# Feed-forward stages of a four-layer metaformer: residual additions moved to GpSimd, the result's rounding to VectorE, a second bank for the centred product in the last stage, zero products on TensorE at the start

## The chip, the cores and the metric

The kernel runs on one core of a Trainium2 chip. The metric is the device time of one execution in microseconds (us), lower is better. Engines are named as in the profile: PE is TensorE (PEld its weight loads), DVE VectorE, ACT ScalarE, POOL GpSimd, SP the engine that issues most DMAs here.

## The reference, cut to what matters

The input is 16 images of 24 channels on 56 x 56 pixels, float32. Four layers follow one another. Each has a mixer (attention in windows, a state-space block, a scan in four directions, a row LSTM) and a feed-forward block:

```python
x = x + mixer(_ln_c(x))                 # normalised over the channels of a pixel, eps 1e-6
t = _to_tokens(x)
h = relu(_qlinear(_ln_t(t), W1, b1))    # 24 -> 96; _ln_t: over the channels too, eps 1e-5
t = t + _qlinear(h, W2, b2)             # 96 -> 24
# _qlinear: operands rounded to 8-bit floats (5 exponent bits, 2 of mantissa), product and sum to float16
```

## The kernel before

All four layers are one program. `x` (tile `all_x`) stays in SBUF for the whole run: four groups of 24 channels lie on partitions 0, 32, 64 and 96, and four images follow one another along each, 12,544 columns in all. `feed_forward_phase` runs once for each layer, after its mixer, which has left its result in device memory (`mixed`, or `by_image` in layer 2). Each feed-forward stage walks over the 12,544 columns in 32 chunks of N = 392. The first three stages (layers 1 to 3) end with the channel norm for the next mixer, which goes to `normed` in device memory; the fourth stage (`last`) stores `x` itself as the output.

The engines each run an order written out by hand, in slots: slot s works on the first step of chunk s, the hidden layer of chunk s-1, the second product of chunk s-2 and the closing norm of chunk s-3. Slots 0 to 2 and the last four are written out, the ones between are a hardware loop over four slots. Semaphores count chunks: a wait for `added` c+1 waits for the addition of chunk c. The steps by their lines:

- SP stores what is finished (`store`, four DMAs, lines 231 and 237) and then loads the mixer's result for the chunk that is six further on (`load`, line 220, four DMAs of 36.8 KB, `AHEAD` = 6, in four buffers).
- DVE adds the mixer's result to `x` (`add_mixed`, L308). PE subtracts the mean (`subtract_mean`, L418, into PSUM tile `xc_ff`, or `xc_ln` for the closing norm). ACT squares (L362), PE averages (`variance`, L425, into `var_ff`, or `ps_y` for the closing norm), ACT takes a logarithm (L368) and an exponential (L372). DVE multiplies and rounds to 8 bits (`quantize`, L285).
- PE makes the hidden layer in two halves (L436), ACT rounds each to float16 (`round_hidden`, L379), DVE adds the bias and rectifies (`rectify`, L292) and rounds to 8 bits (`quantize_hidden`, L303).
- PE makes the second product (L449, into `ps_y`), ACT rounds it to float16 (`round_result`, L386), DVE adds the bias (`add_bias`, L321) and adds the result to `x` (`update`, L314).
- In stages 1 to 3, PE, ACT, PE, ACT, ACT and DVE (`norm`, L330, tile `staged`) make the closing norm of chunk s-3.

GpSimd does nothing in these stages. PE waits for the weights and for all preparations before its first product.

Of the kernel before, what the change touches and what calls it, by code (L numbers as in the profile page):

```python
# [125 lines left out]
AHEAD = 6  # L126


def feed_forward_phase(nc, x, mixed_dram, normed_dram, out_dram, w, st, layer, by_image=False):
# [6 lines left out]
    with ExitStack() as ctx:  # L136
# [37 lines left out]
        ff, ln = st.ff, st.ln  # L174

        all_loads = (layer + 1) * 6 * 16
        preps = 12
# [24 lines left out]
        with nc.Block() as block:  # L202
            @block.sync
            def _(sp):

                sp.dma_start(centre[:], w["centre"]).then_inc(st.weights_in, 16)
                sp.dma_start(average[:], w["average"]).then_inc(st.weights_in, 16)
                sp.dma_start(w1f[:], w["ff_w1"][layer]).then_inc(st.weights_in, 16)
                sp.dma_start(w2f[:], w["ff_w2"][layer]).then_inc(st.weights_in, 16)
                sp.dma_start(b1f[:], w["ff_b1"][layer]).then_inc(st.weights_in, 16)  # L210
                sp.dma_start(b2f[:], w["ff_b2"][layer]).then_inc(st.weights_in, 16)

                def load(j, k, b):
# [3 lines left out]
                    for g in range(G):  # L217
                        rows = (mixed_dram[j + g * J, :, k * N:(k + 1) * N] if by_image
                                else mixed_dram[c + g * CHUNKS])
                        sp.dma_start(group_rows(mixed[b], g), rows  # L220
                                     ).then_inc(st.mixed_in[b], 16)

# [18 lines left out]
                sp.wait_ge(st.prepared, prep0 + 1)  # L241
                for k in range(AHEAD):
                    load(0, k, k % UNROLL)
# [13 lines left out]
            def _(dve):  # L257

                for b in range(UNROLL):

                    cleared = dve.memset(mixed[b][:], 0.0)
# [12 lines left out]
                dve.wait_ge(st.prepared, prep0 + 11)  # L274
# [4 lines left out]
                def quantize(c):  # L279
# [5 lines left out]
                    dve.tensor_tensor(xq[:], xc["ff"][:, 0:N], rstd["ff"][:], ALU.mult,  # L285
# [19 lines left out]
                def add_mixed(c, turn, u):  # L305

                    dve.wait_ge(st.mixed_in[u], (turn + (layer * (CHUNKS // UNROLL) + 1)) * G * 16)
                    dve.tensor_tensor(x[:, bass.ds(c * N, N)], x[:, bass.ds(c * N, N)],  # L308
                                      mixed[u][:], ALU.add).then_inc(ff["added"], 1)

                def update(c):

                    dve.wait_ge(ff["biased"], c + 1 + fb)
                    dve.tensor_tensor(x[:, bass.ds(c * N, N)], x[:, bass.ds(c * N, N)],  # L314
                                       yb[:], ALU.add).then_inc(ff["updated"], 1)
# [20 lines left out]
                def slot(s, turn, u, on):  # L336
                    if on[0]:
                        quantize(s)
# [17 lines left out]
            def _(act):  # L356
# [31 lines left out]
                def slot(s, turn, u, on):  # L388
# [4 lines left out]
                    if on[2]:  # L393
                        round_result(s - 2)
# [1966 lines left out]
```

## Time and profile before

| | us |
|---|---|
| median of 3 runs | 3848.09 (3843.79 to 3852.31) |
| the profiled execution's own time | 3854.38 |
| its span in the profile | 3852.5 |
| first feed-forward stage, first to last quantize (start to start) | 835.0 to 999.9 |
| second | 2413.7 to 2577.3 |
| third, within 0.1 us as long as the second | 3157.6 to 3321.1 |
| fourth | 3675.5 to 3839.1 |

The profile is one execution of the whole program, and its span leaves out 1.9 us that the execution's own time has. The share of busy time of an engine over the span says little here, since the four stages that the change touches take about a fifth of it; what matters is how far apart the slots of a stage are, and which chain of waits sets that distance.

### The profile page before, as it was taken

How to read it: one execution, taken by the hardware profiler on the slowest of the kernel's cores; microseconds unless marked ns; L12 is line 12 of the kernel's file. 1: busy time of each engine (PE TensorE's matmuls, PEld its weight loads, DVE VectorE, ACT ScalarE, POOL GpSimd, SP SyncE). 2: the span in 40 equal slices, each digit the busy share in tenths (PEclk: the TensorE clock that was granted, in tenths of full speed). 3: DMA queues.
4: the chain of work that ended last, by engine and by line, in shares of the span. 5: the costliest groups of instructions: out<-in, count | busy, mean ns of one | idle time of the engine just before them, and what ended most of it. 6: DMA issues, size and time to landing. Idle time of an engine off the chain costs nothing. (4 is left out here: it accounts for less than half of the span.)

```text
span 3852.5 us, 71476 instructions
## 1 busy us (share of the span) xinstructions
PE 3198.3 (83%) x20904; PEld 1809.4 (47%) x20904; DVE 2774.0 (72%) x4460; ACT 2555.0 (66%) x4684; POOL 1635.8 (42%) x1502
## 2 busy tenths in 40 slices
PE   5799999978677898989999765877888858688865
PEld 2688888854233343434444321333433324377722
DVE  2566666657408999989999994666999967544456
ACT  4455555559698988989898642785665629644456
POOL 0233333310047888989898863003766730000000
PEclk9899999989898999999999997998999979899979
DMA  4100000012256657574766522220000002410022
GB/s 96 28 14 14 14 14 14 14 27 59 75 140 186 160 165 197 145 200 134 208 160 188 149 64 73 49 51 22 22 21 20 18 22 58 94 39 17 17 54 53
DMA packets 210810, 298.02 MB, mean 77 GB/s; under 512 B 75034, under 2 KB 195150, under 8 KB 210258
## 3 DMA queue, kind: packets, MB, share of 16 engines
q1 hardware_dynamic: 201066, 286.08, 28.7%
q10 hardware_dynamic: 9576, 10.08, 1.1%
q8 instruction: 59, 0.97, 0.1%
q14 instruction: 109, 0.89, 0.1%
HBM read 193.93 MB, written 102.03 MB: 77 GB/s over the span
## 5 line engine op out<-in xcount | busy, mean ns | idle before, releaser
L1586 POOL TENSOR_TENSOR mam_hc<-mam_h,mam_cs 128x896 f32<-128x896 f32 x336 | 703.1, 2093 | 188.0 <-DVE mam_h L1551 87.0
L1551 DVE TENSOR_TENSOR_SCAN mam_h<-mam_a,mam_kept,mam_dbx 128x448 f32<-128x448 f32 x672 | 738.4, 1129 | 24.4 <-ACT mam_a L1437 23.3
L1318 PE MATMUL mam_ps_y<-mam_hc,mam_ident 128*128 128x448 f32 x1344 | 570.3, 558 | 133.1 <-POOL mam_hc L1586 132.9
L1987 POOL TENSOR_TENSOR scan_ch<-scan_h,scan_cs 128x392 f32<-128x392 f32 x256 | 339.8, 1346 | 399.6 <-DVE scan_h L1931 320.6
L1437 ACT ACTIVATE mam_a<-mam_ft,mam_a_neg 128x448 f32<-128x448 f32 x672 | 410.6, 660 | 81.0 <-DVE mam_h L1551 80.3
L1318 PEld LDWEIGHTS mam_ps_y<-mam_hc,mam_ident 128*128 128x128 f32 x1344 | 249.0, 193 | 433.4 <-POOL mam_hc L1586 224.0
L1538 DVE TENSOR_TENSOR mam_dbx<-mam_ps_u,mam_bs 128x448 f32<-128x448 f32 x672 | 381.7, 613 | 35.6 <-DMA mam_bs<-dram_bc 35.6
L766 POOL TENSOR_TENSOR att_prob<-att_prob,att_share 128x588 f32<-128x588 f32 x128 | 151.7, 1185 | 452.0 <-DVE att_share L951 452.0
L418 PE MATMUL f_xc_ff<-all_x,f_centre 128*128 (+1 forms) x256 | 125.9, 575 | 133.1 <-DVE all_x L308 133.1
L886 ACT ACTIVATE att_pt<-att_ps_t 128x512 f32<-128x512 f32 x128 | 76.5, 598 | 209.9 <-PE att_ps_t L827 209.9
L379 ACT ACTIVATE f_h<-f_hid 96x784 f16<-96x784 f32 x256 | 207.1, 811 | 0.0
L1819 PE MATMUL scan_ps_merged<-scan_ch,scan_w_merge 64*128 64x392 f32 x1024 | 203.7, 532 | 4.0 <-POOL scan_ch L1987 3.8
L867 ACT ACTIVATE att_keys<-att_ps_keys 24x392 f32<-24x392 f32 x384 | 186.9, 487 | 22.5 <-PE att_ps_keys L795 19.5
L1807 PE MATMUL scan_ps_in<-scan_xin,scan_w_in 128*128 128x392 f32 x512 | 189.7, 514 | 6.5 <-ACT scan_rest L1880 4.6
L837 PE MATMUL att_ps_out<-att_pt,att_vals 128*24 128x49 f32 x2048 | 189.5, 208 | 2.1 <-ACT att_pt L886 2.1
L839 PE MATMUL att_ps_out<-att_pt,att_vals 128*24 128x49 f32 x2048 | 187.3, 207 | 0.0
L2121 PE MATMUL lstm_ps<-lstm_hs,lstm_w_h 64*128 64x224 f32 x1344 | 143.1, 358 | 50.8 <-DVE lstm_hs L2202 50.8
L803 PEld LDWEIGHTS att_ps_vals<-att_nvals,att_xw 128*64 128x64 f32 x4096 | 130.5, 138 | 75.5 <-issue 75.5
L957 DVE TENSOR_SCALAR att_result<-att_ps_out,att_b_out 24x392 f32<-24x392 f32 x128 | 78.3, 612 | 116.5 <-PE att_ps_out L839 116.5
L814 PE MATMUL att_ps_scores<-att_keys,att_xw 128*64 128x147 f32 x2048 | 157.2, 295 | 2.0 <-ACT att_keys L867 2.0
L1931 DVE TENSOR_TENSOR_SCAN scan_h<-scan_decay_by_column,scan_h,scan_drive_by_column 128x392 f32<-128x392 f32 x112 | 156.6, 1398 | 0.2
L2121 PEld LDWEIGHTS lstm_ps<-lstm_hs,lstm_w_h 64*128 64x128 f32 x1344 | 123.5, 185 | 70.6 <-DVE lstm_hs L2202 70.2
(216 smaller groups left out, 7361.8 us busy)
## 6 DMA issues: line engine op xcount, KB each, us to landing
mam_taps<-normed SPq DMA_DIRECT2D x1008, 43.5 KB
mam_bs<-dram_bc SPq DMA_DIRECT2D x28, 896.0 KB, 14.7
mam_cs<-dram_bc SPq DMA_DIRECT2D x28, 896.0 KB, 16.6
mam_ft<-dram_steps SPq DMA_DIRECT2D x42, 448.0 KB, 4.8
normed<-f_staged SPq DMA_DIRECT2D x384, 38.1 KB
f_mixed<-mixed SPq DMA_DIRECT2D x384, 36.8 KB
dram_gs<-mam_gs SPq DMA_DIRECT2D x56, 224.0 KB, 2.1
mam_gt<-dram_gs SPq DMA_DIRECT2D x56, 224.0 KB, 2.7
```

The lines of the kernel that those rows point to most:

```text
L379: act.activation(h16[:, 2 * a:2 * a + 2, :], hid[a][0:HID, :, 0:N], ACT.Copy).then_inc(ff["hidden16"], 1)
L837: pe.matmul(ps_out[0:C, cols], vals[p][:, win, 0:C], pt[p][:, q, 64 * half:64 * half + T], start=True, stop=False)
L839: mm = pe.matmul(ps_out[0:C, cols], vals[p][:, win, C:2 * C], pt2[p][:, q, 64 * half:64 * half + T], start=False, stop=True)
L1318: mm = pe.matmul(ps_y[p % 2][:, 0:MT], ident[:], hc[t % 2][:, i, :], start=False, stop=(t % 8 == 7 and i == 1))
L1437: act.activation(a[t % 3][:, i, :], ft[p % 2][:, 0, :], ACT.Exp, scale=a_neg[:, at:at + 1]).then_inc(decays, 1)
L1538: dve.tensor_tensor(dbx[:, i, 0:MT], ps_u[:, 0:MT], bs[:, 2 * pair + i, :], ALU.mult).then_inc(driven, 1)
L1551: dve.tensor_tensor_scan(h[:, n % 8, :], a[t % 3][:, i, :], dbx[:, i, 0:MT], kept[:, at:at + 1], ALU.mult, ALU.add).then_inc(scanned, 1)
L1586: pool.tensor_tensor(hc[t % 2][:], h[:, row:row + 2, :], cs[:, 2 * pair:2 * pair + 2, :], ALU.mult).then_inc(weighed, 1)
L1807: pe.matmul(ps_in[i][:, 0:N], w_in[:, i, :], xin[p][:, :, 1:SIDE + 1], start=True, stop=True).then_inc(projected, 1)
L1819: mm = pe.matmul(ps[:, 0:N], w_merge[rows, n, :], ch[rows, n, :], start=(n == 0), stop=(n == DIRS - 1))
L1987: pool.tensor_tensor(out, hd, in_order(cs, 1 - half, d, k), ALU.mult).then_inc(weighed, 1)
L2121: mm = pe.matmul(ps[p][:, pair, half, 0:W], w_h[lanes, tap, pair, :], hs[lanes, :, y, tap:tap + SIDE], start=False, stop=(tap == 2))
```

## The change

Four edits, all in `feed_forward_phase`:

- The two additions to `x` move from DVE to GpSimd: `add_mixed` for chunks 0 to 3, then for each chunk c `update(c)` followed by `add_mixed(c + 4)`.
- `round_result` moves from ACT to DVE, just ahead of `add_bias`.
- In the last stage, where `xc_ln` has no other use, the centred product of even chunks goes to `xc_ff` and of odd chunks to `xc_ln`, and it waits for the quantize of the chunk before the last one (`held` = 1) in place of the last one.
- PE multiplies a tile of zeros (`squares_ln`, cleared by GpSimd, 128 x 128 by 128 x 392, float32) into `ps_y`: five times at its start, twice after the first variance, and twice at the end of slots 0 and 1. It then waits for the two constant matrices alone ahead of the first centred product, and SP issues these and chunk 0's load ahead of the weights.

```diff
+AHEAD_ADDED = 4
+WARM_UP = 5
+        fronts = (xc["ff"], xc["ln"]) if last else (xc["ff"], xc["ff"])
...
+                sp.dma_start(centre[:], w["centre"]).then_inc(basis_in, 16)
+                sp.dma_start(average[:], w["average"]).then_inc(basis_in, 16)
+                sp.wait_ge(st.prepared, prep0 + 1)
+                load(0, 0, 0)
+                sp.dma_start(w1f[:], w["ff_w1"][layer]).then_inc(st.weights_in, 16)
...
-                def add_mixed(c, turn, u):
-
-                    dve.wait_ge(st.mixed_in[u], (turn + (layer * (CHUNKS // UNROLL) + 1)) * G * 16)
-                    dve.tensor_tensor(x[:, bass.ds(c * N, N)], x[:, bass.ds(c * N, N)],
-                                      mixed[u][:], ALU.add).then_inc(ff["added"], 1)
...
+                def round_result(c):
+
+                    dve.wait_ge(ff["summed"], c + 1 + fb)
+                    dve.tensor_copy(y16[:], ps_y[:, 0:N]).then_inc(ff["summed16"], 1)
...
+            @block.gpsimd
+            def _(pool):
+                pool.memset(squares["ln"][:], 0.0).then_inc(warm, 1)
+
+                def add_mixed(c):
+
+                    pool.wait_ge(st.mixed_in[c % UNROLL],
+                                 (c // UNROLL + (layer * (CHUNKS // UNROLL) + 1)) * G * 16)
+                    pool.tensor_tensor(x[:, c * N:(c + 1) * N], x[:, c * N:(c + 1) * N],
+                                       mixed[c % UNROLL][:], ALU.add).then_inc(ff["added"], 1)
+
+                def update(c):
+
+                    pool.wait_ge(ff["biased"], c + 1 + fb)
+                    pool.tensor_tensor(x[:, c * N:(c + 1) * N], x[:, c * N:(c + 1) * N],
+                                       yb[:], ALU.add).then_inc(ff["updated"], 1)
+
+                for c in range(AHEAD_ADDED):
+                    add_mixed(c)
+                for c in range(CHUNKS):
+                    update(c)
+                    if c + AHEAD_ADDED < CHUNKS:
+                        add_mixed(c + AHEAD_ADDED)
...
-                def round_result(c):
-
-                    act.wait_ge(ff["summed"], c + 1 + fb)
-                    reached(act, ff["biased"], c + fb)
-                    act.activation(y16[:], ps_y[:, 0:N], ACT.Copy).then_inc(ff["summed16"], 1)
...
+                def multiply_zeros(times):
+                    for _ in range(times):
+                        pe.matmul(ps_y[:, 0:N], squares["ln"][:, 0:P], squares["ln"][:],
+                                  start=True, stop=True)
...
-                    reached(pe, s[reader], c + base)
-                    pe.matmul(xc[name][:, 0:N], centre[:], x[:, bass.ds(c * N, N)],
+                    held = int(last)
+                    if base > 0 or not isinstance(c, int) or c > held:
+                        pe.wait_ge(s[reader], c + base - held)
+                    to = fronts[u % 2] if name == "ff" else xc[name]
+                    pe.matmul(to[:, 0:N], centre[:], x[:, bass.ds(c * N, N)],
                               start=True, stop=True).then_inc(s["centred"], 1)
```

On VectorE, one slot of the hardware loop in stages 1 to 3 stands before as follows (L308 and L314 are the two additions; ISA and REGISTER_ALU rows are address arithmetic).

```order
L285 TENSOR_TENSOR f_xq<-f_xc_ff,f_rstd_ff 128x392
L308 ISA
L308 TENSOR_TENSOR all_x<-all_x,f_mixed 128x392
L290 REGISTER_ALU
L292 TENSOR_SCALAR f_hr<-f_h,f_b 96x784
L321 TENSOR_SCALAR f_yb<-f_y,f_b 128x392
L314 ISA
L314 TENSOR_TENSOR all_x<-all_x,f_yb 128x392
L290 REGISTER_ALU
L292 TENSOR_SCALAR f_hr<-f_h,f_b 96x784
L302 MEMSET f_gate 128x1
L303 CAST f_h<-f_hr 96x1568
```

The same slot on VectorE after the change.

```order
L292 TENSOR_TENSOR f_xq<-f_xc_ff,f_rstd_ff 128x392
L297 ISA
L299 TENSOR_SCALAR f_hr<-f_h,f_b 96x784
L315 CAST f_y<-f_ps_y 128x392
L39 REGISTER_ALU
L321 TENSOR_SCALAR f_yb<-f_y,f_b 128x392
L297 REGISTER_ALU
L299 TENSOR_SCALAR f_hr<-f_h,f_b 96x784
L309 MEMSET f_gate 128x1
L310 CAST f_h<-f_hr 96x1568
```

Both additions are gone, and one rounding from PSUM (`f_y<-f_ps_y`) has come in between the first rectify and the bias. GpSimd, which had no instruction here, begins a stage after the change like this (its own row order).

```order
L354 MEMSET f_squares_ln 128x392
L360 TENSOR_TENSOR all_x<-all_x,f_mixed 128x392 x4
L366 TENSOR_TENSOR all_x<-all_x,f_yb 128x392
L360 TENSOR_TENSOR all_x<-all_x,f_mixed 128x392
L366 TENSOR_TENSOR all_x<-all_x,f_yb 128x392
L360 TENSOR_TENSOR all_x<-all_x,f_mixed 128x392
```

The addition of chunk c+4 stands right behind the update of chunk c, so each of the two is queued behind what the other waits for. On PE the start of a stage after the change is this (L426 are the zero products, one row for each run of them).

```order
L426 MATMUL f_ps_y<-f_squares_ln 128x392 x5
L441 MATMUL f_xc_ff<-all_x,f_centre 128x392
L448 MATMUL f_var_ff<-f_squares_ff,f_average 128x392
L426 MATMUL f_ps_y<-f_squares_ln 128x392 x2
L441 MATMUL f_xc_ff<-all_x,f_centre 128x392
L448 MATMUL f_var_ff<-f_squares_ff,f_average 128x392
L426 MATMUL f_ps_y<-f_squares_ln 128x392 x2
L456 MATMUL f_hid<-f_gate_bf 128x2
```

Before, the centred product was PE's first instruction of a stage; now five products of zeros stand ahead of it, and two more stand between a chunk's variance and the hidden layer of the chunk before it, in slots 0 and 1.

## Rows read from the trace of the kernel before

**Rows 1.** Timeline, stage 1, one slot: start, length, engine, line [idle before it]
```profile
901.44 0.57 DVE L285 TENSOR_TENSOR f_xq<-f_xc_ff,f_rstd_ff 128x392 fp8e5<-128x392 f32 x1
...
901.92 0.56 DVE L308 TENSOR_TENSOR all_x<-all_x,f_mixed 128x392 f32 x1
...
902.62 0.92 PE L418 MATMUL f_xc_ff<-all_x,f_centre 128*128 x2 [0.50 <-DVE all_x L308]
...
904.22 0.90 PE L425 MATMUL f_var_ff<-f_squares_ff,f_average 128*128 128x392 f32 x2
...
906.59 0.57 DVE L285 TENSOR_TENSOR f_xq<-f_xc_ff,f_rstd_ff 128x392 fp8e5<-128x392 f32 x1
```

**Rows 2.** Source line L285 (quantize), stages 1, 2 and 4: ns min/median/max, first and last start
```profile
L285 DVE TENSOR_TENSOR f_xq<-f_xc_ff,f_rstd_ff x32: 561/567/568, 835.0 to 999.9; 128x392 fp8e5<-128x392 f32 x32
L285 DVE TENSOR_TENSOR f_xq<-f_xc_ff,f_rstd_ff x32: 560/567/568, 2413.7 to 2577.3; 128x392 fp8e5<-128x392 f32 x32
L285 DVE TENSOR_TENSOR f_xq<-f_xc_ff,f_rstd_ff x32: 561/567/567, 3675.5 to 3839.1; 128x392 fp8e5<-128x392 f32 x32
```

**Rows 3.** Timeline, last stage: one slot and part of its chain
```profile
3763.58 0.56 DVE L308 TENSOR_TENSOR all_x<-all_x,f_mixed 128x392 f32 x1
...
3767.88 0.80 ACT L379 ACTIVATE f_h<-f_hid 96x784 f16<-96x784 f32 x1
...
3768.62 0.56 DVE L308 TENSOR_TENSOR all_x<-all_x,f_mixed 128x392 f32 x1
```

**Rows 4.** Timeline, stage 1: closing norm, stores and loads, two slots
```profile
900.38 0.57 DVE L330 TENSOR_TENSOR f_staged<-f_xc_ln,f_rstd_ln 128x392 f32<-128x392 f32 x1 [0.54 <-ACT f_rstd_ln L372]
...
901.13 1.88 SPq L237 DMA_DIRECT2D normed<-f_staged  x4
...
903.27 1.84 SPq L220 DMA_DIRECT2D f_mixed<-mixed  x4
...
907.76 0.92 PE L418 MATMUL f_xc_ff<-all_x,f_centre 128*128 x2 [0.54 <-DVE all_x L308]
...
908.52 0.82 PE L425 MATMUL f_ps_y<-f_squares_ln,f_average 128*128 128x392 f32 x2
...
910.67 0.57 DVE L330 TENSOR_TENSOR f_staged<-f_xc_ln,f_rstd_ln 128x392 f32<-128x392 f32 x1 [0.43 <-ACT f_rstd_ln L372]
```

**Rows 5.** DMA issues by tile: count, KB each, median us from issue to landing
```profile
f_centre<-in_centre SPq DMA_DIRECT2D x4, 64.0 KB, 1.8
```

**Rows 6.** Groups by line: count | busy us, mean ns | idle before it
```profile
L292 DVE TENSOR_SCALAR f_hr<-f_h,f_b 96x784 f16<-96x784 f16 x256 | 105.7, 414 | 3.3 <-ACT f_h L379 2.2
L321 DVE TENSOR_SCALAR f_yb<-f_y,f_b 128x392 f16<-128x392 f16 x128 | 40.0, 313 | 9.2 <-ACT f_y L386 9.1
L303 DVE CAST f_h<-f_hr 96x1568 fp8e5<-96x1568 f16 x128 | 123.8, 967 | 5.4
```

**Rows 7.** Source lines of mixers 2 and 3, where POOL and DVE work together: ns min/median/max
```profile
L1987 POOL TENSOR_TENSOR scan_ch<-scan_h,scan_cs x256: 1007/1214/1870, 2648.2 to 3135.9; 128x392 f32<-128x392 f32 x128
L1931 DVE TENSOR_TENSOR_SCAN scan_h<-scan_decay,scan_h,scan_drive x112: 1001/1591/2027, 2652.6 to 3129.9; 128x392 f32<-128x392 f32 x112
L1551 DVE TENSOR_TENSOR_SCAN mam_h<-mam_a,mam_kept,mam_dbx x672: 1110/1131/1148, 1164.5 to 2344.8; 128x448 f32<-128x448 f32 x168
```

**Rows 8.** Timeline, mixer 3: a POOL product and two DVE scans beside it
```profile
2706.38 1.20 POOL L1987 TENSOR_TENSOR scan_ch<-scan_h,scan_cs 128x392 f32<-128x392 f32 x1 [0.91 <-DVE scan_h L1931]
2707.00 2.34 DVE L1931 TENSOR_TENSOR_SCAN scan_h<-scan_decay,scan_zero,scan_drive 128x392 f32<-128x392 f32 x2 [0.24 <-DVE scan_drive L1945]
```

**Rows 9.** The page's costliest groups: the same POOL line, with its mean
```profile
L1987 POOL TENSOR_TENSOR scan_ch<-scan_h,scan_cs 128x392 f32<-128x392 f32 x256 | 339.8, 1346 | 399.6 <-DVE scan_h L1931 320.6
```

**Rows 10.** Timeline, start of stage 1
```profile
829.81 1.65 PE L418 MATMUL f_xc_ff<-all_x,f_centre 128*128 128x392 f32 x2 [9.21 <-DVE all_x L308]
```

**Rows 11.** Windows at the start of stage 1: busy us by engine, granted clock, DMA
```profile
840.00:850.00 10.00, 8.09 (x23) 3.60 (x22) 4.05 (x11) 5.24 (x9) 0.00 (x0) 0.50 0.00 0
853.00:856.00 3.00, 2.39 (x11) 1.23 (x8) 2.15 (x7) 2.78 (x6) 0.00 (x0) 1.00 0.00 0
```

## The prediction before the change was run

> **What bounds the kernel now.** The four feed-forward stages are the only code that changes. I read the timeline of a settled slot of stage 1 first. From one quantize of VectorE to the next are 5.15 us, and the reader can follow who waits for whom: quantize at 901.44, the mixer's addition of the next chunk at 901.92, the centred product at 902.62 (PE had been idle 0.50 us for that addition), the variance at 904.22, and the next quantize at 906.59 [rows 1]. So a stage moves at the pace of one chain that runs through every engine, and the addition is a link of it. Two gaps are used below. An operation on VectorE can start about 0.09 us before the one ahead of it ends (901.44 + 0.57 against 901.92), and PE starts 0.14 us after VectorE ends (901.92 + 0.56 against 902.62) [rows 1]. In the last stage a slot takes 3768.62 - 3763.58 = 5.04 us [rows 3].
>
> Over a whole stage, the source line of quantize gives first and last start: 164.9 us in stage 1, 163.6 in stage 2 (the third is like it), 163.6 in the last, each for 31 slots [rows 2]. That is more than 31 settled slots, because a stage starts slowly: TensorE has half its clock, 1.2 GHz, in the window 840 to 850 and the whole of it from 853 on [rows 11], and the first centred product takes 1.65 us where a settled one takes 0.92 [rows 10, 1].
>
> A second chain doesn't set the pace today, but lies close under it. SP issues the loads of chunk c+6 behind the stores of chunk c, which wait for the closing norm of chunk c. In the timeline the norm starts at 900.38, its stores at 901.13, the loads at 903.27 [rows 4]. The loads' own landing isn't shown; a 64 KB load lands 1.8 us after its issue [rows 5], and the last of four goes out about 1.5 us after the first (they take 1.84 together [rows 4]). So the buffer is full at about 903.27 + 1.5 + 1.8 = 906.6, and the addition that reads it stands a slot behind 901.92, at 907.1. That is half a microsecond of slack, no more.
>
> **Additions to GpSimd: what leaves.** In stages 1 to 3 the centred product now follows the quantize alone: it starts 0.57 + 0.14 = 0.71 us after it in place of 1.18, so this chain would shrink from 5.15 to 4.68 us. ACT also loses one rounding, which had no part in the chain.
>
> **What GpSimd costs.** The trace has no such addition, but it has a product of two 128x392 float32 tiles on POOL: 1.01 us at least, median 1.21, mean 1.35, up to 1.87 [rows 7, 9]. The spread comes from waits: a VectorE scan with both inputs in SBUF takes 1.00 us alone and up to 2.03 beside POOL, that is its own time and POOL's, while a scan with one input in PSUM stays within 1.11 to 1.15 in 672 cases [rows 7]. So two such operations exclude each other. How much of POOL's time counts: two scans that start at 2707.00 take 2.34 us in place of 2 x 1.00 - 0.09 = 1.91, so the first was held until 2707.43, 0.15 us before POOL's end at 2707.58 [rows 8]. I take 1.01 us for each addition, waits apart, of which it shuts VectorE out for 0.85.
>
> Which VectorE operations of these stages are shut out is not shown. Quantize, the norm and the new rounding touch PSUM. Rectify (0.41 us), bias (0.31) and the 8-bit cast (0.97) [rows 6] have all their data in SBUF, but one input only. Lower end: they pass freely, like the scan of mixer 2. Upper end: they are held as the scans of mixer 3 are. I take the upper end, because those scans are the row with all data in SBUF, and because rectify and bias move data fast: 392 elements more (784 against 392) cost 0.10 us, where one element per ns would cost 0.39 [rows 6].
>
> The Trainium skill (SBUF — State Buffer, "Who interferes with whom") says that casts and tensor-scalar operations that use both port pairs of VectorE exclude GpSimd, as do operations with two SBUF inputs, and that whichever comes second waits. The scans here agree with its second half, 2.03 against 1.00 us. By it the sum is the same as mine; by the PSUM row alone it would be that of the first rival.
>
> **Stages 1 to 3, the new chain.** GpSimd's queue holds the addition of chunk c+4 behind the update of chunk c, and PE needs it one slot later. So it isn't four slots ahead: it is at the landing of its load, about where VectorE's addition was, and takes 0.45 us longer. Following that load: norm to stores 0.75, stores to loads 2.14, loads to landing 3.3 [rows 4, 5]; then the addition, which holds the first rectify for about 0.9 with its start; rectify 0.33 (start to start); rounding 0.55 + 0.14 (the quantize, also 392 columns out of PSUM, takes 0.57); bias and hand-over to GpSimd 0.46; the update, which holds the second rectify 0.85; rectify 0.41 + 0.14; cast 0.88; then the norm, two chunks on. Sum 10.85 us for two slots: 5.42 a slot, 0.2 to 0.3 more than now. Without the holding, the same loads lead through the addition (1.01 + 0.14) to the centred product, the closing variance 0.76 behind it and the norm 2.15 behind that [rows 4]: 10.25, or 5.13 a slot. So the loads alone eat up what the shorter chain offers.
>
> In slots 0 and 1 the two zero products (0.82 us each at the whole clock, by the closing variance of 0.82 [rows 4]) stand ahead of the hidden layer that the next quantize waits for: 0.71 + 1.60 + 0.73 + 1.65 + 1.05 (my estimate for both halves) = 5.7 us each. A stage is then 2 x 5.7 + 29 x 5.42 = 168.6; six chunks are loaded ahead, and the last six load nothing, which I put at 2.5 us: 166.1, against 164.9, 163.6 and 163.6. That is +1.2, +2.5, +2.5, and 0.5 at each end, where rounding and update (0.55 + 1.01, and 0.48 + 0.57 as they were) stand bare: **+7.7 us** in all.
>
> **Last stage.** With two banks the centred product doesn't wait for the quantize before it, and there is no norm. The stores wait for the update, so loads are early. The loop left runs through GpSimd twice in two slots: hidden rounding of ACT to rectify 0.80 + 0.14, rectify 0.33, rounding 0.69, bias 0.46, update 0.85, the cast that it held 0.80 until the next addition gets in, and from an addition to the hidden rounding 3767.88 - 3763.58 = 4.30 [rows 3], with 0.45 for GpSimd's slower addition. Sum 8.82, or 4.41 a slot for 5.04. The stage: 2 x 5.2 + 29 x 4.41 = 138.3 against 163.6, with 0.5 for the end: **-24.8 us**.
>
> **Start of a stage.** Five zero products take 8.2 us at the low clock, 4.1 at the high one. They start about when the constants' DMAs go out, near 824, so the first centred product comes between 828.3 and 832.4 in place of 829.81 [rows 10], and the chain behind it takes 3.9 us in place of 5.2 if the clock has risen (1.65 for 0.92 twice). I take three of the five at the low clock: 830.6 and 3.9, a gain of 0.5 us; with bounds of 2.8 gained and 2.6 lost, four times. I take **-1 us** for the four.
>
> **Sum:** +7.7 - 24.8 - 1 = -18.1 us. The profiled execution took 3854.38 us, 1.88 more than its span and 6.3 more than the median of the runs. Its time becomes 3836; beside the median, 3848.09 - 18.1 = **3830 us**.
>
> **Rivals.**
> - *VectorE isn't held by GpSimd* (chance 0.17). For it speaks the PSUM scan that never stretched. Stages 1 to 3: 11.4 + 29 x 5.13 - 2.5 = 157.7, so -7.2, -5.9 and -5.9, with 1.5 for the ends. The last: its loop without the cast and with the update at 1.01, then the addition right behind: 0.94 + 0.33 + 0.69 + 0.46 + 1.01 + 4.75 = 8.18, 4.09 a slot, 129 us, -34. Sum -53: 3795 us.
> - *GpSimd's additions are dearer* (chance 0.13; slower). The update mixes float16 with float32, which no POOL row shows. Each two-slot loop holds two additions, so a slot grows by what one addition grows: 0.34 us at the mean of 1.35. Over 120 slots that is +41: 3871 us. It decides from 18/120 = 0.15, that is from 1.16 us an addition on, and the median of the POOL row is 1.21, though there it includes waits.
> - *The zero products don't raise the clock* (chance 0.07). Then slots 0 to 2 run at 1.2 GHz as today, and the products of zeros cost 1.65 each in front of the chain: 2.6 at the start and about 5 in the slots, four times, +30 against my sum: 3860 us.
> - The rest (0.63) is my forecast, 3812 to 3846.
>
> **How the numbers follow.** A difference of less than 0.2%, 7.7 us, can't be told from none. The likeliest case gives 3830. The holding is uncertain by 0.1 us a slot, 12 us. Faster by over 0.2% are nearly all of my case (0.59) and the first rival: 0.76. Same: 0.11, from my case's slow edge and the second rival near 1.16. Slower: 0.13, the rest of the two slower rivals. The range takes in most of the first rival and the slow edge: 3794 to 3852.
>
> **What would show it.** POOL rows for the two additions at 1.0 to 1.2 us alone; rectify and cast stretched by up to 0.85 in the source view, or else still at 0.41 and 0.97, which would be the first rival. In stages 1 to 3 the additions on POOL released by the load's DMA, and slots of 5.3 to 5.5; in the last stage slots of 4.3 to 4.5. A granted clock of 1.00 within 10 us of the stage's start. The prediction fails if the loads land earlier than 1.8 us, if POOL's order of who comes first turns out otherwise, or if the clock falls during the last stage.

## The result, and the profile after

The changed kernel takes 3792.91 us (median of four runs, 3788.24 to 3801.28), the kernel before 3848.39 (median of four runs, 3843.79 to 3852.31). The ratio is 0.9854, 95% interval 0.9833 to 0.9876: 55 us faster, where 18 were predicted, and 1 us below the range. The profiled execution took 3801.28 us with a span of 3799.7, against 3852.5 before, so 52.8 us of span are to be accounted for. Comparisons rest on executions in the fast state; one of e1's six (3901.19 us) was in the slow one, which moves its median by 0.2 us.

The source view of quantize (now L292) gives each stage as [rows 2] did: ns min/median/max, first and last start. Shown are stages 1 and 2, then the last one, whose even and odd chunks have a tile each. (The same instruction has other line numbers in other kernels: quantize is L292 here, L298 in e4 and e8, L303 in e9.)

```profile
L292 DVE TENSOR_TENSOR f_xq<-f_xc_ff,f_rstd_ff x32: 555/567/568, 832.0 to 990.9; 128x392 fp8e5<-128x392 f32 x32
L292 DVE TENSOR_TENSOR f_xq<-f_xc_ff,f_rstd_ff x32: 554/567/568, 2398.4 to 2557.9; 128x392 fp8e5<-128x392 f32 x32
...
L292 DVE TENSOR_TENSOR f_xq<-f_xc_ff,f_rstd_ff x16: 565/567/568, 3648.8 to 3780.6; 128x392 fp8e5<-128x392 f32 x16
L292 DVE TENSOR_TENSOR f_xq<-f_xc_ln,f_rstd_ff x16: 561/566/567, 3653.2 to 3785.0; 128x392 fp8e5<-128x392 f32 x16
```

| stretch | before | after | difference |
|---|---|---|---|
| first to last quantize, stage 1 | 164.9 | 158.9 | -6.0 |
| stage 2 | 163.6 | 159.5 | -4.1 |
| stage 3 | 163.5 | 159.5 | -4.0 |
| last stage | 163.6 | 136.2 | -27.4 |
| SP's first DMA to first quantize, four stages | 11.7, 11.9, 12.0, 11.9 | 9.2, 10.0, 9.6, 9.0 | -9.5 |

That makes -51.0 of -52.8. The last stage's gain is close to the one forecast (-25.3 for this stretch). Stages 1 to 3 gained 14 us where I had a loss of 6.2, and the starts gained 9.5 where I had 1. For the ends of the stages I had +2.0 in all; behind the last quantize are 1.2 us more than before. What is left, 3 us less, lies outside the stages, where the code is the same in both kernels.

**A slot of stage 1.** The timeline after the change, two slots: start, length, engine, line, then idle time before it and what ended it.

```profile
899.52 1.01 POOL L360 TENSOR_TENSOR all_x<-all_x,f_mixed 128x392 f32<-128x392 f32 x1 [1.85 <-DMA f_mixed<-mixed]
...
899.58 0.57 DVE L292 TENSOR_TENSOR f_xq<-f_xc_ff,f_rstd_ff 128x392 fp8e5<-128x392 f32 x1
900.16 0.59 DVE L299 TENSOR_SCALAR f_hr<-f_h,f_b 96x784 f16<-96x784 f16 x1
...
900.67 0.92 PE L441 MATMUL f_xc_ff<-all_x,f_centre 128*128 x2 [0.45 <-POOL all_x L360]
900.67 0.55 DVE L315 CAST f_y<-f_ps_y 128x392 f16<-128x392 f32 x1
...
901.26 0.32 DVE L321 TENSOR_SCALAR f_yb<-f_y,f_b 128x392 f16<-128x392 f16 x1
...
901.43 0.82 PE L448 MATMUL f_ps_y<-f_squares_ln,f_average 128*128 128x392 f32 x2
...
901.50 0.42 DVE L299 TENSOR_SCALAR f_hr<-f_h,f_b 96x784 f16<-96x784 f16 x1
...
901.66 1.04 POOL L366 TENSOR_TENSOR all_x<-all_x,f_yb 128x392 f32<-128x392 f32 x1 [1.13 <-DVE f_yb L321]
901.96 1.57 DVE L310 CAST f_h<-f_hr 96x1568 fp8e5<-96x1568 f16 x1
...
902.91 0.53 ACT L394 ACTIVATE f_rstd_ln<-f_logvar_ln 128x392 f32<-128x392 f32 x1
...
903.58 0.57 DVE L330 TENSOR_TENSOR f_staged<-f_xc_ln,f_rstd_ln 128x392 f32<-128x392 f32 x1
...
904.41 1.01 POOL L360 TENSOR_TENSOR all_x<-all_x,f_mixed 128x392 f32<-128x392 f32 x1 [1.70 <-DMA f_mixed<-mixed]
...
908.62 0.56 DVE L330 TENSOR_TENSOR f_staged<-f_xc_ln,f_rstd_ln 128x392 f32<-128x392 f32 x1
...
909.64 1.01 POOL L360 TENSOR_TENSOR all_x<-all_x,f_mixed 128x392 f32<-128x392 f32 x1 [2.16 <-DMA f_mixed<-mixed]
```

The mixer's addition waits for its load (14 of 14 times from 890 to 960 in its source view), and PE still waits for the addition, not for the quantize. Holding, that is a VectorE operation drawn out by a GpSimd one beside it, is there in three sizes: the cast takes 1.57 us beside the update (0.97 alone, [rows 6]); the first rectify 0.59 in place of 0.42; in the next slot the second rectify takes 1.10. But the addition starts 0.06 us before the quantize, which reads PSUM and isn't held (0.57). Only its last 0.37 us lie beside the rectify, and 0.17 of that shows. From the addition at 899.52 to the norm at 903.58 are 4.06 us, from the next, at 904.41, to 908.62 are 4.21. My sum had 4.66 for the same way; over the 20 norms from 883 to 981 it is 4.16 on average. From a norm to the addition two slots on are 909.64 - 903.58 = 6.06 (I had 6.19).

Two ways lead from the addition to the norm, and here they end together. On VectorE the held cast ends at 901.96 + 1.57 = 903.53. Through PE and ACT, the last step before the norm ends at 902.91 + 0.53 = 903.44, and that way is the one that the prediction gave for the case without holding: 1.01 + 0.14 + 0.76 + 2.15 = 4.06 us, which is what this slot took. In the next slot VectorE is the later of the two, by the 4.21 - 4.06 = 0.15 us that show.

**A slot of the last stage.** GpSimd's addition stands right behind the update, and the cast takes its turn between them.

```profile
3703.00 1.03 POOL L366 TENSOR_TENSOR all_x<-all_x,f_yb 128x392 f32<-128x392 f32 x1 [1.20 <-DVE f_yb L321]
3703.29 1.57 DVE L310 CAST f_h<-f_hr 96x1568 fp8e5<-96x1568 f16 x1
...
3704.00 1.74 POOL L360 TENSOR_TENSOR all_x<-all_x,f_mixed 128x392 f32<-128x392 f32 x1
```

The update (1.03) holds the cast, and then the cast holds the addition: 1.74 us in place of 1.01. Whichever comes first keeps the other out, as the prediction had it.

**The start.** Timeline, then three windows of the start of stage 1: busy us by engine (PE, PEld, DVE, ACT, POOL), granted clock, DMA share, GB/s.

```profile
823.16 5.25 PE L426 MATMUL f_ps_y<-f_squares_ln 128*128 128x392 f32 x10 [3.13 <-POOL f_squares_ln L354]
...
828.25 0.82 PE L441 MATMUL f_xc_ff<-all_x,f_centre 128*128 128x392 f32 x2
```

```profile
824.00:826.00 2.00, 2.00 (x4) 1.01 (x3) 1.33 (x8) 0.00 (x0) 0.00 (x0) 0.50 0.50 123
826.00:828.00 2.00, 2.00 (x6) 1.12 (x5) 0.00 (x0) 0.00 (x0) 1.01 (x1) 0.73 0.66 204
828.00:830.00 2.00, 1.35 (x5) 0.59 (x4) 1.03 (x6) 0.50 (x1) 0.00 (x0) 1.00 0.39 80
```

The granted clock goes from 0.50 (1.2 GHz) to 1.00 (2.4 GHz) behind PE's work on zeros, and the first real product takes 0.82 us in place of 1.65 [rows 10]. The five products (ten passes) took 5.25 us together. I had priced each at 1.65 at the low clock, 8.2 for five.

### The profile page after: what moved, and what is told of

It is laid out like the page before. It is cut to its first block and busy times, and to the rows that moved or that the text cites. A ratio compares the mean times of both kernels' runs of the same rounds, so it can differ in the third digit from the quotient of the medians.

```text
span 3799.7 us, 71340 instructions
## 1 busy us (share of the span) xinstructions
PE 3217.6 (85%) x20992; PEld 1810.3 (48%) x20992; DVE 2814.0 (74%) x4332; ACT 2504.7 (66%) x4556; POOL 1918.1 (50%) x1762
## 5 line engine op out<-in xcount | busy, mean ns | idle before, releaser
L1564 DVE TENSOR_TENSOR mam_dbx<-mam_ps_u,mam_bs 128x448 f32<-128x448 f32 x672 | 380.9, 610 | 39.3 <-DMA mam_bs<-dram_bc 39.3
L366 POOL TENSOR_TENSOR all_x<-all_x,f_yb 128x392 f32<-128x392 f32 x128 | 128.2, 1002 | 239.6 <-DVE f_yb L321 239.6
L360 POOL TENSOR_TENSOR all_x<-all_x,f_mixed 128x392 f32<-128x392 f32 x128 | 152.5, 1191 | 180.4 <-DMA f_mixed<-mixed 123.4
L310 DVE CAST f_h<-f_hr 96x1568 fp8e5<-96x1568 f16 x128 | 173.3, 1354 | 5.4
```

Source lines behind the costliest of these rows:

```text
L310: dve.tensor_copy(h8[p][:], hr[:], saturate=False).then_inc(ff["hidden8"], 1)
L1564: dve.tensor_tensor(dbx[:, i, 0:MT], ps_u[:, 0:MT], bs[:, 2 * pair + i, :], ALU.mult).then_inc(driven, 1)
```

## The experiments

Every time is a median; its ratio is to the kernel before, which ran again beside each group (3847 to 3851 us), and isn't exactly the quotient of the two medians. Stage lengths are from first to last quantize in the one profiled execution of each run.

Outside these stages and their starts the 14 profiled executions take between 3131.5 and 3149.6 us, though the mixers' code is the same: between the first and the second stage alone 1387.1 (e1) to 1402.0 us (before) pass, and the mixer there waits for one of its loads (mam_bs) 29.6 us in e1 and 39.3 in the changed kernel. So small differences are read from the stages here, not from the totals.

### The change without one of its parts

**e1: no zero products.** All eleven of a stage left out.

```diff
-WARM_UP = 5
+WARM_UP = 0
-                    if isinstance(s, int) and s < 2:
-                        multiply_zeros(2)
-                multiply_zeros(2)
```

> The changed kernel without any zero product; its order of loads at the start stays. Theory (the zero products raise TensorE's clock early and cost less than that gives): in the first stage the first quantize comes about 1 us later, slots 0 to 2 are again near 6.7, 6.7 and 5.3 us in place of 5.40, 5.40 and 4.62, so each of the four stages loses 4 to 5 us: 3808 to 3813 us against 3793. Rival (the gain at the start of a stage is from the earlier load and the earlier first product, and the zero products only stand in the way): slots 0 and 1 lose the 0.7 us each that the zero products take, and the time is 3787 to 3793.

Measured: 3805.74 us, ratio 0.9907 (0.988 to 0.9934), 13 us slower than the changed kernel, with runs that spread from 3799 to 3829. The starts are 4.5 us longer together, stages 1 to 3 8.1 us (162.9, 162.2, 161.1), the last 2.1 us shorter (134.1): 10.5 us in all, less than the 16 to 20 expected. In stage 1 the first three slots take 6.30, 6.28 and 5.32 us, with the granted clock at 0.50 until 846 (5.40, 5.40 and 4.62 in the changed kernel at 1.00; 6.70, 6.70 and 5.31 before). So the zero products pay in three stages and cost a little in the last, where two slots of 3.93 and 3.97 us became 4.45 and 4.69 with them.

**e2: one bank in the last stage.**

```diff
-        fronts = (xc["ff"], xc["ln"]) if last else (xc["ff"], xc["ff"])
+        fronts = (xc["ff"], xc["ff"])
-                    held = int(last)
+                    held = 0
```

> The changed kernel with one bank for the centred product in the last stage too. Theory (the two-slot loop through GpSimd, about 4.40 us a slot, lies just under the loop through quantize and the centred product, about 4.65): slots of 4.6 to 4.7, the last stage from 136.2 to 142 to 144 us from first to last quantize: 3799 to 3801 us. Rival 1 (the second bank is what brought the last stage from 5.04 down): back to about 5.0 a slot, +19: 3812 us. Rival 2 (the second bank does nothing): 3793 us.

Measured: 3810.79 us, ratio 0.9905 (0.9888 to 0.9922). The last stage takes 145.9 us in place of 136.2, in settled slots of 4.56 to 4.76, as the theory had them; the others are as they were. The total is 10 us above the theory's, more than the stage explains. Its source view of quantize, the reader of the bank, shows who waited for it: PE's centred product, 31 times.

```profile
L292 DVE TENSOR_TENSOR f_xq<-f_xc_ff,f_rstd_ff x32: 561/567/567, 3648.0 to 3793.9; 128x392 fp8e5<-128x392 f32 x32
...
  PE f_xc_ff L441: 20.8, 31
```

So the second bank is worth 9.6 us in this stage, with the additions on GpSimd.

**e4: both additions back on VectorE**, behind the quantize as before; rounding, banks and zero products as in the change.

```diff
 # VectorE's slot
                         quantize(s, u)
+                    if has_next(s):
+                        add_mixed(s + 1, turn + int(u == UNROLL - 1), (u + 1) % UNROLL)
...
                         add_bias(s - 2)
+                        update(s - 2)
```

> The changed kernel with both additions back on VectorE, where they stood before; chunk 0's addition stands ahead of the weights' casts. The rounding on VectorE, the second bank and the zero products stay. Theory (the gain of stages 1 to 3 comes from the shorter chain without the additions, that of the last stage from the second bank): stages 1 to 3 at 5.2 us a slot, that is 161 to 163 us from first to last quantize in place of 159 to 160, the last at 4.5 to 4.6 a slot in place of 4.40: 3800 to 3806 us. Rival (GpSimd is what made the last stage fast): the last stage back near 5.0 a slot: 3818 us or more. Rival 2 (holding costs more than the move gives): 3785 us or less.

Measured: 3835.82 us, ratio 0.9969 (0.9955 to 0.9982), 30 us above the theory's range; its rival came, a last stage near 5.0 a slot. All that the change gained in the stages is gone: 163.1, 165.3, 165.4 and, in the last, 161.4 us. In each of the last three, 1.6 to 1.7 us are the clock's: slot 1 takes 7.4 to 7.5 us there in place of 5.80 in stage 1, and the granted clock has fallen to 0.60 and 0.54 in the windows 2402 to 2404 and 2404 to 2406 of stage 2 (the variance at 2402.59 takes 1.65 us), to 0.50 and 0.52 in stages 3 and 4. The rest is the slots' own. The last stage's timeline shows why two banks don't help here:

```profile
3719.57 0.57 DVE L298 TENSOR_TENSOR f_xq<-f_xc_ln,f_rstd_ff 128x392 fp8e5<-128x392 f32 x1
3720.06 0.56 DVE L326 TENSOR_TENSOR all_x<-all_x,f_mixed 128x392 f32 x1
...
3720.77 0.92 PE L443 MATMUL f_xc_ff<-all_x,f_centre 128*128 x2 [1.03 <-DVE all_x L326]
...
3724.61 0.57 DVE L298 TENSOR_TENSOR f_xq<-f_xc_ff,f_rstd_ff 128x392 fp8e5<-128x392 f32 x1
```

The product has its bank free, but its input is written behind the quantize, so it waits for that quantize all the same, and a slot is 5.04 us as before.

**e5: the result's rounding back on ACT.**

```diff
-                        round_result(s - 2)     # VectorE, ahead of add_bias
+                    if on[2]:                   # ScalarE, between the halves of the hidden rounding
+                        round_result(s - 2)
```

> The changed kernel with the result's rounding back on ACT (between the two hidden roundings), the additions still on GpSimd. Theory (ACT has no slack left in stages 1 to 3: its eight operations fill a slot of 4.9 to 5.1 us): slots of 5.2 to 5.3 there, 161 to 165 us a stage in place of 159 to 160; in the last stage 4.5 to 4.8 a slot in place of 4.40: 3803 to 3815 us. Rival (VectorE with GpSimd's holding is the bound, so that taking 0.5 us from VectorE helps): stages 1 to 3 under 157 us each, 3785 us or less.

Measured: 3811.33 us, ratio 0.9908 (0.9892 to 0.9923). The total lies in the theory's range, but not for its reason: stages 1 to 3 don't change (158.8, 159.9, 159.5, where 161 to 165 were expected), so ACT sets no pace there; the last takes 150.0 us, 13.8 more. Moving the rounding pays only where the slot is short.

**e6: only the new start and the zero products**, e4 with rounding and banks undone too.

> The kernel before with the start part of the change alone: zero products, constants and chunk 0's load ahead of the weights, chunk 0's addition ahead of the weights' casts; additions on VectorE, rounding on ACT, one bank. Theory (the start part is worth about 2.4 us ahead of the first quantize and 1 to 2 in the first slots, four times): settled slots as before (5.15 and 5.04), first slots 5.8, 5.8, 5.0: 3831 to 3837 us against 3847. Rival (the zero products give back what they save): 3842 to 3850 us.

Measured: 3838.21 us, ratio 0.997 (0.996 to 0.9981): 163.4, 164.2, 164.2, 161.1 us for the stages, starts of 10.5, 10.4, 9.5 and 8.4. This part alone brings 12 us, 1 us less than the range expected. One of the first two slots of each stage takes 7.4 to 7.5 us in place of 5.8; in stage 1 the granted clock falls to 0.63 and 0.51 there (836 to 840).

### Who sets the pace in stages 1 to 3

**e3: loads issued ahead of the stores.** SP issues the loads of chunk c+6 before it waits for the closing norm of chunk c, in stages 1 to 3.

```diff
-                        store(j * K + k, j, k, k % 2)
-                        load_ahead(j, k)
+                        if last:
+                            store(j * K + k, j, k, k % 2)
+                        load_ahead(j, k)
+                        if not last:
+                            store(j * K + k, j, k, k % 2)
```

> The changed kernel, where SP issues in stages 1 to 3 the loads of chunk c+6 ahead of the stores of chunk c, so that they no longer wait for the closing norm. Theory L (in stages 1 to 3 the loads set the pace: the mixer's addition on GpSimd waits for its load in every slot, 14 of 14 in the stretch 890 to 960): that wait goes, the slots fall from 5.1 to about 4.9, where ACT is full, and the kernel gains 12 to 18 us: 3775 to 3781 us. Theory H (GpSimd's holding of rectify and cast sets the pace): no gain, 3790 to 3800 us, with the additions on GpSimd earlier in the slot and the slots as long as before.

Measured: 3807.09 us, ratio 0.9897 (0.9881 to 0.9913), stages of 162.3, 162.5 and 162.5: 3 us longer each than with late loads, which neither theory had. The theory that the loads alone set the pace fell. With the load in time the addition follows the update at once, as the timeline shows:

```profile
902.70 0.92 POOL L371 TENSOR_TENSOR all_x<-all_x,f_yb 128x392 f32<-128x392 f32 x1 [3.36 <-DVE f_yb L326]
...
903.10 0.74 DVE L304 TENSOR_SCALAR f_hr<-f_h,f_b 96x784 f16<-96x784 f16 x1 [0.48 <-ACT f_h L406]
903.58 1.13 POOL L365 TENSOR_TENSOR all_x<-all_x,f_mixed 128x392 f32<-128x392 f32 x1
903.88 1.67 DVE L315 CAST f_h<-f_hr 96x1568 fp8e5<-96x1568 f16 x1
```

The update holds the rectify, the addition holds the cast, and every cast from 880 to 980 takes 1.66 to 1.67 us. In the changed kernel the wait for the load had kept the mixer's addition apart from the update before it by chance, mostly with 1.3 to 2.3 us of idle time between them.

**e7: the same, and the addition kept off the cast.** One wait more on GpSimd: the addition of chunk c+4 starts when the hidden cast of chunk c+1, which PE needs soon, is done.

```diff
                     if c + AHEAD_ADDED < CHUNKS:
+                        pool.wait_ge(ff["hidden8"], c + 2 + fb)
                         add_mixed(c + AHEAD_ADDED)
```

> The changed kernel with the loads ahead of the stores in stages 1 to 3, as in the run before, and with one wait more in all stages: GpSimd adds the mixer's result of chunk c+4 only after VectorE has cast chunk c+1 to 8 bits. In the run with the loads first, update and addition stood back to back on GpSimd and the cast took 1.67 us in place of 0.97. Theory H (which GpSimd operation meets which VectorE operation sets the pace of stages 1 to 3): the addition now runs beside the norm and the quantize, which touch PSUM, the cast is back at 0.97 to 1.6, and a stage takes 154 to 157 us from first to last quantize in place of 162.5: 3775 to 3785 us. Rival (the order of SP's DMAs lengthened the slots by itself): 162 us a stage again, 3800 us or more.

Measured: 3778.68 us, ratio 0.9821 (0.9802 to 0.984), stages of 152.8, 152.8 and 152.7, even less than expected. Source view of the cast, 880 to 980:

```profile
L315 DVE CAST f_h<-f_hr x21: 967/968/969, 880.1 to 978.2; 96x1568 fp8e5<-96x1568 f16 x21
...
  POOL all_x L365: 27.5, 21
```

GpSimd's addition (L365) now waits for the cast each time (21 of 21), and no cast is held. So one wait more on GpSimd took 28 us out of e3; its stages 1 to 3 are 29 us shorter. The last stage lost 3.1 us by it against the change (139.3 for 136.2).

### Is it GpSimd, or the place of the addition?

**e8: both additions on VectorE, the mixer's addition ahead of the quantize.** It differs from e4 in the order of two instructions; the edit is against e4.

```diff
-                        quantize(s, u)
                     if has_next(s):
                         add_mixed(s + 1, turn + int(u == UNROLL - 1), (u + 1) % UNROLL)
+                    if on[0]:
+                        quantize(s, u)
```

> The changed kernel with both additions on VectorE, and the mixer's addition of chunk s+1 one place earlier than before the change: ahead of the quantize of chunk s, not behind it. No GpSimd operation is left beside VectorE in the slots. Theory (what counts is that the addition leaves the chain from quantize to the centred product, on whichever engine): stages 1 to 3 at 4.8 to 5.0 us a slot, the last at 4.3 to 4.6: 3785 to 3795 us, as good as the change or better. Rival (VectorE is full with two additions, rounding and casts, so that only GpSimd can take them): stages 1 to 3 at 5.2 or more, the last at 4.9 or more: 3815 us or more.

Measured: 3794.06 us, ratio 0.9865 (0.9846 to 0.9884): the time of the changed kernel, without GpSimd, and 42 us less than e4, of which about 5 are the falls of e4's clock. The last stage takes 132.1 us, stages 1 to 3 160.9, 161.4 and 161.0, in slots of 4.8 and 5.5 to 6.1 us in turn. In the longer ones VectorE waits for the load, with the quantize queued behind:

```profile
899.86 0.57 DVE L326 TENSOR_TENSOR all_x<-all_x,f_mixed 128x392 f32 x1 [1.07 <-DMA f_mixed<-mixed]
...
900.35 0.56 DVE L298 TENSOR_TENSOR f_xq<-f_xc_ff,f_rstd_ff 128x392 fp8e5<-128x392 f32 x1
```

**e9: e8 with the loads ahead of the stores.**

> The run before with both additions on VectorE (the mixer's one ahead of quantize), and the loads ahead of the stores in stages 1 to 3. There, slots went 4.8, 5.6, 4.8, 5.6 in stages 1 to 3. Theory (every second slot waited for a load that stood behind the stores; without GpSimd nothing holds VectorE): all slots near 4.8 to 4.9, 149 to 152 us a stage in place of 161, the last stage as before at 132: 3758 to 3768 us. Rival (the alternation is VectorE running out of time): 158 us or more a stage, 3785 us or more.

Measured: 3759.7 us, ratio 0.9788 (0.9769 to 0.9808), the best of all; its stages:

```profile
L303 DVE TENSOR_TENSOR f_xq<-f_xc_ff,f_rstd_ff x32: 556/566/568, 829.9 to 981.3; 128x392 fp8e5<-128x392 f32 x32
...
L303 DVE TENSOR_TENSOR f_xq<-f_xc_ff,f_rstd_ff x16: 556/557/565, 3607.7 to 3735.8; 128x392 fp8e5<-128x392 f32 x16
L303 DVE TENSOR_TENSOR f_xq<-f_xc_ln,f_rstd_ff x16: 556/562/567, 3612.2 to 3739.7; 128x392 fp8e5<-128x392 f32 x16
```

The edit that made stages 1 to 3 9.4 us longer in e3 (487.3 us together for 477.9) makes them 27.9 us shorter here (455.4 for 483.3). So the loads did set a pace, once nothing held VectorE: settled slots of stages 1 to 3 are now all at 4.8 to 4.9 us.

**e11: e9 and one addition per chunk on GpSimd that nobody needs**, a tile of its own to itself, released with the update.

```diff
+                    pool.wait_ge(ff["biased"], c + 1 + fb)
+                    pool.tensor_tensor(spare[:], spare[:], spare[:], ALU.add).then_inc(warm, 1)
```

> The run with additions on VectorE and loads first, and beside it one GpSimd addition a slot that nobody needs: a spare 128x392 float32 tile to itself, released by the biased result of each chunk as the update is. It tells the price of the holding alone, since no engine waits for its result. Theory (a GpSimd operation keeps VectorE's operations with all data in SBUF waiting): this time VectorE's own additions, the second rectify and the cast can be held, up to 0.85 us a slot; VectorE has 0.3 to 0.5 us to spare, so slots grow by 0.1 to 0.5 us in stages 1 to 3 and in the last: 12 to 60 us over the run without it. Rival (the longer rectify and cast rows come from something else): no slot changes by more than 0.03 us and no row of VectorE is stretched.

Measured: 3822.67 us, ratio 0.9933 (0.9917 to 0.9948): 63 us more than e9, for an operation that no engine waits for. Groups by line of e9, whole program (count | busy us, mean ns | idle):

```profile
L310 DVE TENSOR_SCALAR f_hr<-f_h,f_b 96x784 f16<-96x784 f16 x256 | 106.7, 417 | 4.1 <-ACT f_h L410 1.9
L337 DVE TENSOR_TENSOR all_x<-all_x,f_yb 128x392 f16 (+1 forms) x128 | 72.6, 567 | 14.3 <-DVE f_yb L344 9.7
```

The same of e11:

```profile
L311 DVE TENSOR_SCALAR f_hr<-f_h,f_b 96x784 f16<-96x784 f16 x256 | 140.7, 550 | 2.4 <-ACT f_h L417 1.9
L388 POOL TENSOR_TENSOR f_spare<-f_spare 128x392 f32<-128x392 f32 x128 | 130.7, 1021 | 595.8 <-DVE f_yb L345 595.8
L338 DVE TENSOR_TENSOR all_x<-all_x,f_yb 128x392 f16 (+1 forms) x128 | 114.3, 893 | 14.3 <-DVE f_yb L345 9.7
```

VectorE's rectify and update took 34.0 and 41.7 us more, 75.7 together, and most of it came out at the end. The four stages are 10.2, 12.1, 12.0 and 18.9 us longer (161.5, 164.3, 163.9, 151.0 against 151.3, 152.2, 151.9, 132.1), 53 us together, or 0.43 us a slot. The two profiled spans differ by 68.2 us; the 15 left lie outside the stages, 7.8 of them between the first and the second, where runs differ by up to 15 us anyway. So the price shown is 53 us.

**e10: e9 with zero products at the start only** (the ones after the first variance and in slots 0 and 1 left out).

> The same without the zero products behind the first variance and in slots 0 and 1; the five ahead of the first centred product stay. Theory (those in the slots stand in front of the hidden layer, 1.3 us a slot, and the clock is already up): slots 0 and 1 fall from 5.39 to 4.7 to 4.9 where the clock stays up, 1 us a stage, 3 to 5 us in all. Rival (without them the clock falls back in the first slots, as the run without any zero product showed it low): slots 0 to 2 at 6.3, 6.3, 5.3, and 4 to 8 us more in all.

Measured: 3761.01 us, ratio 0.9781 (0.9764 to 0.9798). The stages are 0.7 to 1.7 us shorter (150.6, 151.1, 151.2, 130.4), the starts 0.8 us longer together, and the total can't be told from e9's. In stage 1 the first two slots take 5.53 and 4.41 us without the products, 5.39 and 5.40 with them. Without them the granted clock falls to 0.50 from 834 to 836, so that slot 0 is no shorter, and is back at 1.00 in slot 1. The products hold the clock up, but take more time than that brings, and aren't worth having in this version.

**e12: the changed kernel once more.**

> The changed kernel itself once more, on the same chip as these, for comparison: 3788 to 3802 us, stages of 159, 160, 160 and 136 us.

Measured: 3799.76 us, ratio 0.9877 (0.9862 to 0.9893), stages of 158.6, 159.6, 159.5 and 136.3. Two groups of runs of one kernel stand 7 us apart, with the same stages within 0.3 us. So totals of runs that weren't side by side say nothing about differences of that size, and the stages tell much finer ones. e3 is 14 us slower than the changed kernel by the first group and 7 by this one, e1 13 and 6: what is said of these two rests on their stages.

## Why the prediction was right in direction and wrong in size

- **What bounds the kernel: right.** The chain through the addition set the pace. e4 and e8 show it best: the same work on the same engines, the addition behind or ahead of the quantize, 3835.82 and 3794.06 us, with about 5 of the 42 us from the clock.
- **The price of GpSimd's additions: right.** I took 1.01 us, waits apart; measured were 1.013 in the median for the mixer's addition and 1.033 for the update, whose second input is float16, and at least 1.007 and 0.922. The rival of dearer additions is refuted.
- **VectorE is held: right as a mechanism.** Casts of 1.57 to 1.67 us beside GpSimd against 0.97, and e11's 53 us, leave no room for the first rival's "they pass freely". That its number, 3795, came out is in part luck: it had 12.1 us too much gain in the stages (-19.0 and -34.6 for -14.1 and -27.4) and, with the starts as I had them, 8.5 us too little there. In part it isn't: its 5.13 us a slot for stages 1 to 3 came close to the measured 5.11, because the way that it followed, 4.06 us from addition to norm, was there beside the held one. The Trainium skill (SBUF — State Buffer, "Who interferes with whom") says that the pair of ports shared by the two engines belongs to whichever operation comes first, for the whole instruction. The last stage's 1.57 and 1.74 us agree with it in both directions, but for the last 0.13 to 0.14 us of the operation that holds: the cast has 0.97 us of its own, so it got going at 3703.29 + 0.60 = 3703.89, and the update ended at 3704.03.
- **The step that failed: "then the addition, which holds the first rectify for about 0.9 with its start" and the sum of 10.85 us for two slots** (stages 1 to 3). I laid the holding end to end on the path: 4.66 us from addition to norm. Measured are 4.06 and 4.21, on average 4.16, hardly more than the 4.06 of the way without holding, and the two slots shown take 4.06 + 6.06 = 10.12 us. The addition runs beside the quantize, so the rectify lost 0.17 and not 0.9. The second rectify or the cast is held, 0.6 to 0.7 us, where I had 0.85; and VectorE hands over to itself in 0.04 us (900.67 + 0.55 against 901.26), where I added 0.14 for each. In stage 1 the two first slots took 5.40 for 5.7, -0.6, and the other 29 took 5.11 on average for 5.42, -9.1: that leads from the 168.6 of the sum to the 158.9 measured. The relief of 2.5 at the end of a stage, an estimate that no row showed, is 0.8 us in that average (the last three slots took 4.90, 4.84 and 4.77).
- **"So the loads alone eat up what the shorter chain offers": right for the change, only half the story.** The addition was released by its load 14 of 14 times. But taking the wait away made it slower (e3), since the wait also spaced GpSimd's two additions. e7 and e9 show what was behind: without the collision, in either way, the same loads give 151 to 153 us a stage.
- **Start of a stage: the term was mis-sized.** Five zero products cost 5.25 us, inside my bounds of 4.1 and 8.2, where I took 6.6: 1.65 us was the length of a lone product at the low clock, while in a row their weight loads follow one another every 0.65 us, two to a product, and the clock rose on the way. They also began 0.4 us behind the first DMA, not 0.7, and the chain behind took 3.72 us for 3.9. My own working gave 0.5 us a start, of which the sum took 1 for four. Together the starts gained 9.5 us for 1 forecast. The rival that the products of zeros don't raise the clock is refuted (0.73, then 1.00 from 828 on; 0.50 until 846 in e1).
- **Last stage: right.** 4.38 us a slot for 4.41 forecast, in turns of 4.0 and 4.7 as a loop over two slots has them, and 136.2 us for 138.3; the first two slots took 4.45 and 4.69 for 5.2. e2, e4 and e5 show that each part counts: without the second bank 145.9, without the rounding's move 150.0, with the additions behind the quantize again 161.4. That they must be on GpSimd isn't so: e8 has 132.1.
- **Sum of the errors:** stages 1 to 3 -14.1 for +6.2, that is -20.3; starts -9.5 for -1, -8.5; last stage -27.4 for -25.3, -2.1. Together -30.9, which turns the -20.1 that I had for these stretches into the -51.0 of the table. The range was set too narrow on this side: the lower end of the holding was a case of its own, with its stage forecast taken whole, and no case had the holding present but off the path.

## What to carry to other kernels

Before moving an operation to another engine, try its place in the order it has: here an addition ahead of the quantize rather than behind it gave all that GpSimd gave, and with earlier loads 33 us more (29 of them in the stages and their starts). Price an operation on GpSimd also by what it holds on VectorE beside it: here one that nobody waited for cost 0.43 us a slot, while the changed kernel's VectorE operations that read PSUM were never drawn out. So choose its neighbours, if need be with one wait more. Then look whether what is held lies on the path at all: here it had a second way of nearly the same length beside it. Undo such a change part by part, since a late load can be what keeps two operations from colliding, and an edit's sign can turn with the other parts (loads first: +9 us in stages 1 to 3 with GpSimd, -28 without).

## What the runs showed of the hardware

- VectorE's 8-bit cast of 96x1568 float16 took 0.97 us alone and 1.57 to 1.67 beside an addition of GpSimd; its rectify of 96x784 float16 took 0.41 alone and up to 1.25; its addition of float32 and float16, both in SBUF, 0.57 alone and 0.89 on average in e11. Quantize, norm and the rounding, which all read PSUM, stayed at 0.55 to 0.57 in the changed kernel. For cast and rectify, which have one input, this was open before.
- GpSimd's addition of 128x392 took 1.01 us with two float32 inputs, 1.03 with a float32 and a float16 one (0.92 at the least), and up to 1.74 behind a cast.
- Products of zeros raised the granted clock from 0.50 to 1.00 as real ones do (0.50, 0.73, 1.00 in three windows of 2 us). The clock can fall again behind them: to 0.50 in slot 0 of e10 (834 to 836), and to 0.60 and 0.54 in slot 1 of e4's second stage, where the next variance took 1.65 us in place of 0.90.
